# Two VectorE clears moved to GpSimd, and two ScalarE conversions moved out of the way of the second block's features, in an attention and mixture-of-experts kernel

## The chip, the cores and the metric

One core of a Trainium2 chip runs the kernel. The metric is the time of one execution on the device, in microseconds (us).

## What is computed

```
x = L0_attn_x                                   # 4 x 2048 x 256, f32
x = x + attention(layernorm(x))                 # 16 heads of 16: elu(q)+1, elu(k)+1, causal linear attention, Wo
x = x + moe(layernorm(x))                       # 8 experts, top 2 by router, hidden 512, exact gelu

# attention, token by token, with state s and z kept per batch row and head:
s = s + k_i (outer) v_i;   z = z + k_i
out_i = (q_i s) / (q_i z + 1e-6)

# moe: logits = x . router_w; top 2, softmax over the two
y = gelu(x . w1[e] + b1[e]) . w2[e] + b2[e], weighted by the two probabilities and added
```

## The kernel before, in words

The attention is done in 16 steps of 128 positions; a step holds these positions of all 4 batch rows, so 4 x 128 tokens. Every f32 operand of a matmul is split in two f16 numbers, a **high** part (ScalarE rounds it: the helpers whose names end in `hi` or `high`) and a **low** part (value minus high, on VectorE or GpSimd: `lo` or `low`), and a product is three matmuls. After the steps comes a second phase, in which gathered token rows go through their experts' two layers tile by tile; the change doesn't touch it.

Each engine runs its own program, written out by hand in the order in which it is to run, and waits on semaphores for the others. All of them walk the same list of calls (`iterations`):

```
            body(0, 0)
            body(0, 1, back=False)
            body(0, 1, front=False)
            for c in range(2, END):
                body(0, c)
```

A `body` has a **front** part, the features of step c (normalise, transpose, project to q, k and v, exponentials, splits), and a **back** part, the attention of step c-1 (scores, weighted values, state, output projection, residual, second normalisation). From c = 2 on they are interleaved. The first ones stand alone: block one is `body(0, 0)` (the features of step 0), the **second block** is `body(0, 1, back=False)` (the features of step 1), and after it stands the **back of step 0**, `body(0, 1, front=False)` with nothing of a front beside it.

What the change and the prediction name, with the lines of the kernel before:

- On ScalarE: `x_hi` (L990) copies the transposed x from the PSUM banks pF to xT. `kn_rows` (L975) copies turned k rows. `v_high` (L1024) writes the high half of v into vhl, and GpSimd's `v_low` (L1799) subtracts it and writes the low half. `w1_high` (L1048) writes the high half of one 512-column slice of the first expert weight w1 (staged in w1raw) into w1s; VectorE's `w1_low` (L1419) writes its low half. `feature_in` and `feature_exp` (L998, L999, L1004) turn a projected bank into et and lt; `qk_high` (L1017) rounds a finished feature. `turned_copies` (L1029, L1030) copies turned output weights. `score_hi` (L984) rounds a bank of scores into ahl. `out_hi` (L1035) rounds the turned attention output. `normalise` is L947.
- On VectorE: `x_lo` (L1279), `feature` (L1425), `low` (L1429), `values` (L1351, v from its bank), `score_lo` (L1274, the low half of a score bank), `norm_moments` (L1241 and L1243), `norm1_shift` (L1259 and L1260), `attention` (L1298 to L1305: denominators and the division into at), `state_part` (L1314), `residual` (L1333, L1344, L1247). Two clears stand at the end of block one: pads (L1464), which holds padding rows that are written to DRAM some 70 us later, and state (L1465), which is the attention state.
- On TensorE: `first_transposes` (L583), `project` (L564, pF from xT and was), `scores` (L650 and L654), `attend` (L669 with the state, L675 with the scores, then the state's product into pU), `out_transpose` (L695), `out_project` (L564 into pA). `attend` of step 0 waits for the cleared state (`zero_set`), for all four low score banks of its batch row (`sc_lo`) and for the low half of v (`v_lo`).
- On GpSimd: `rstd` (L1755, a power of four numbers per partition), `v_low`, `state_add` (L1783). Its start clears a part of qst (L1868).
- SyncE's queue issues the loads. The load of the second w1 slice (L493) waits for `w1_lo` of the first, since both use w1raw.

In the second block and in the back of step 0 no other front or back work lies beside these orders: in the second block ScalarE has the features alone, in the back of step 0 it has the scores.

Of the kernel before, what the change touches and what calls it, by code (L numbers as in the profile page):

```python
# [105 lines left out]
def build(nc, x, wqkvo, bqk, bv, bo, rw, w1, b1, w2, b2, cf, ch, cb, cm, out):  # L106
# [5 lines left out]
    with ExitStack() as ctx:  # L112
# [820 lines left out]
        def _(act):  # L933
# [27 lines left out]
            def body(j, c, front=True, back=True):  # L961
# [117 lines left out]
                if c == STEPS + 1:  # L1079

                    w2_high(0)
                    w2_high(1)
                if fr and c == 1:
                    v_high(0)
                    w1_high(0)
                if fr:
# [23 lines left out]
                if bk:  # L1110
                    out_hi(s, 0)
                    score_hi(1, 2)
                    score_hi(1, 3)
                if fr:
                    feature(3)
                    qk_high(2)
# [6 lines left out]
                if fr:  # L1123
                    qk_high(3)
                if bk:
                    score_hi(2, 1)
# [101 lines left out]
        def _(dve):  # L1228
            V = nc.vector
# [32 lines left out]
            def body(j, c, front=True, back=True):  # L1262
# [171 lines left out]
                if fr and c < 2:  # L1434
# [25 lines left out]
                    low(3)  # L1460
                    if c == 1:
                        w1_low(0)
                    if c == 0:
                        V.memset(pads[:].rearrange("p s d -> p (s d)"), 0.0).then_inc(pads_set, 1)  # L1464
                        V.memset(state[:].rearrange("p a b c -> p (a b c)"), 0.0).then_inc(zero_set, 1)  # L1465
                        V.tensor_copy(dummy_token[:], cfs[:, C_PAD + 2:C_PAD + PADS]).then_inc(pads_set, 1)
                        dve.wait_ge(pads_set, 1)
                        for n in range(2):
                            V.tensor_copy(pads[:, n, TOKEN:TOKEN + 1], cfs[:, C_PAD + n:C_PAD + n + 1]).then_inc(pads_set, 1)
                        dve.wait_ge(lgx0_ps, 1)  # L1470
                        logit_x(0, pR[:, LGX0:LGX0 + B * E])
# [63 lines left out]
                if ahead:  # L1535
                    norm1_stats(i + 1, 3)
                    norm_moments(i + 1, st1, mv1, ve1, (ln1_st, ln1_mv, ln1_ve))
                if c == STEPS:
                    router_slots()
# [210 lines left out]
        def _(pool):  # L1750
# [6 lines left out]
            def body(j, c, front=True, back=True):  # L1757
# [44 lines left out]
                if fr and c < 2:  # L1802

                    if c == 0:
                        rstd(1, ve1, rs1, ln1_ve, ln1_rs)
                    else:
                        v_low(0)
# [61 lines left out]
            pool.wait_ge(pow_set, 1)  # L1869
            rstd(0, ve1, rs1, ln1_ve, ln1_rs, lg[:, 0, 0:B])  # L1870
            pool.wait_ge(cf_in, 16)
            pool.wait_ge(consts_in, CONSTS)
# [75 lines left out]
```

## Time and profile before

| | |
|---|---|
| median of 3 runs | 1023.68 us (1023.34 to 1023.85) |
| profiled execution, its own time | 1024.11 us |
| its span in the trace | 1022.3 us |
| TensorE (PE) matmuls | 917.8 us, 90% of the span |
| VectorE (DVE) | 754.4 us, 74% |
| ScalarE (ACT) | 681.3 us, 67% |
| GpSimd (POOL) | 621.1 us, 61% |
| granted TensorE clock, mean | 0.976 of full speed |

Block one ends at about 25 us of the span, the second block at about 40 us, and the back of step 0 at about 65 us; the attention goes on to about 565 us. Busy time is summed over instructions and says nothing of which of them another waited for; that is read from the rows in order of time. An instruction's own duration is a little longer than the distance to the next one on its engine, since the end of one overlaps the start of the next: where instructions follow each other without a wait, one takes the distance.

### The profile page before, as it was taken

What the parts mean: (1) busy time and instruction counts of PE and PEld (TensorE: products, weight loads), DVE (VectorE), ACT (ScalarE), POOL (GpSimd) and SP (SyncE); (2) the same over time, 40 slices, a digit from 0 to 9 for tenths busy, and PEclk for the clock granted to TensorE, in tenths of its full rate; (3) what the DMA queues carried; (4) which work ended last, traced back from release to release, by engine and by line L of the source; (5) the groups of instructions that cost most, each with busy time, mean ns of one, the idle gap of its engine ahead of it and who ended that gap; (6) DMA issues with size and microseconds to landing.
All of it is one profiled execution on the core that took longest, in us unless ns stands there. A gap on an engine that the chain in (4) does not pass through costs nothing. (4 is left out here: it accounts for less than half of the span.)

```text
span 1022.3 us, 33747 instructions
## 1 busy us (share of the span) xinstructions
PE 917.8 (90%) x10786; PEld 745.5 (73%) x10787; DVE 754.4 (74%) x2281; ACT 681.3 (67%) x1296; POOL 621.1 (61%) x564
## 2 busy tenths in 40 slices
PE   6799899899989999999987659899999999999995
PEld 3577677767777677767766338678999999999994
DVE  6689788988888888888887556456666666666663
ACT  8778888888878988888875315445555555555552
POOL 2135776777677767786673644447655565656565
PEclk9999999999999999999999769999999999999998
DMA  7626744554555354644441743435655656555554
GB/s 195 199 79 204 244 129 150 153 175 125 152 150 176 125 154 142 186 132 144 141 150 47 279 137 70 68 61 96 93 97 89 98 89 98 89 98 88 95 91 51
DMA packets 102584, 131.32 MB, mean 128 GB/s; under 512 B 15056, under 2 KB 89296, under 8 KB 101648
## 3 DMA queue, kind: packets, MB, share of 16 engines
q1 hardware_dynamic: 74336, 92.54, 32.2%
q0 software_dynamic: 25680, 35.01, 18.7%
q10 hardware_dynamic: 2464, 2.38, 0.7%
q8 instruction: 65, 1.06, 0.5%
q14 instruction: 39, 0.32, 0.1%
HBM read 64.29 MB, written 65.60 MB: 127 GB/s over the span
## 5 line engine op out<-in xcount | busy, mean ns | idle before, releaser
L1906 POOL DMA_INDIRECT out<-yt,to_token x135 | 216.7, 1605 | 176.6 <-DVE yt L1744 80.2
L1274 DVE SCALAR_TENSOR_TENSOR ahl<-pS,ahl 128x512 f16<-128x512 f32 x240 | 161.2, 682 | 42.4 <-ACT ahl L984 38.4
L984 ACT ACTIVATE ahl<-pS 128x512 f16<-128x512 f32 x240 | 142.2, 599 | 49.5 <-PE pS L654 32.2
L1789 POOL DMA_INDIRECT expert_in<-xn,cur x128 | 131.6, 1028 | 30.2 <-issue 26.0
L1196 ACT ACTIVATE g<-pS,b1s 128x256 f32<-128x256 f32 (+1 forms) x140 | 57.3, 462 | 94.6 <-PE pS L564 94.6
L564 PE MATMUL pS<-gT,w1s 128*128 128x256 f16 (+1 forms) x840 | 97.3, 272 | 4.3 <-DVE gT L1703 3.5
L564 PE MATMUL pF<-w2s,ghl 128*128 x816 | 95.6, 273 | 2.4 <-issue 1.5
L1710 DVE TENSOR_TENSOR ghl<-g,ghl 128x1024 f16<-128x1024 f32 (+1 forms) x68 | 83.0, 1221 | 19.4 <-ACT ghl L1221 12.6
L564 PE MATMUL pU<-w2s,ghl 128*128 x804 | 94.2, 273 | 1.9 <-issue 1.5
L564 PE MATMUL pF<-xT,was 128*128 128x512 f16 x384 | 92.8, 379 | 3.0 <-DVE xT L1279 2.9
L1783 POOL TENSOR_TENSOR state<-state,ut 128x272 f32<-128x272 f32 x64 | 49.9, 780 | 73.4 <-DVE ut L1314 72.5
L675 PE MATMUL pO<-vhl,ahl 128*128 128x17 f16 x3072 | 90.2, 171 | 4.2 <-DVE ahl L1274 3.4
L675 PEld LDWEIGHTS pO<-vhl,ahl 128*128 128x128 f16 x3072 | 88.3, 96 | 7.4 <-DVE ahl L1274 4.2
L564 PEld LDWEIGHTS pS<-gT,w1s 128*128 x840 | 80.9, 99 | 16.1 <-issue 5.6
L654 PE MATMUL pS<-qst,kst 128*128 128x256 f16 x480 | 92.0, 274 | 0.0
L650 PE MATMUL pS<-cbs 128*128 128x384 bf16 x240 | 79.1, 329 | 11.1 <-DVE ahl L1274 7.4
L564 PEld LDWEIGHTS pF<-w2s,ghl 128*128 128x128 f16 x816 | 79.3, 98 | 13.2 <-issue 3.7
L564 PEld LDWEIGHTS pU<-w2s,ghl 128*128 128x128 f16 x804 | 78.2, 98 | 12.4 <-issue 2.9
L1196 ACT ACTIVATE g<-pO,b1s 128x256 f32<-128x256 f32 (+1 forms) x72 | 29.1, 459 | 77.4 <-PE pO L564 73.3
L1221 ACT ACTIVATE ghl<-g 128x1024 f16<-128x1024 f32 (+1 forms) x68 | 72.0, 1059 | 0.1
L564 PEld LDWEIGHTS pF<-xT,was 128*128 128x128 f16 x384 | 36.2, 98 | 35.9 <-DVE xT L1279 3.3
L654 PEld LDWEIGHTS pS<-qst,kst 128*128 128x128 f16 x480 | 47.2, 98 | 20.2 <-issue 0.3
(226 smaller groups left out, 2170.2 us busy)
## 6 DMA issues: line engine op xcount, KB each, us to landing
xg<-expert_in SPq DMA_DIRECT2D x64, 260.0 KB
qk_parts<-qkhl SPq DMA_DIRECT2D x64, 256.0 KB, 2.1
qst<-qk_parts SPq DMA_DIRECT2D x192, 64.0 KB
kst<-qk_parts SPq DMA_DIRECT2D x96, 128.0 KB
xs<-x SPq DMA_DIRECT2D x16, 512.0 KB
out<-x SPq DMA_DIRECT2D x16, 512.0 KB
w1raw<-w SPq DMA_DIRECT2D x16, 256.0 KB
w2raw<-w SPq DMA_DIRECT2D x4, 1024.0 KB, 7.2
```

The source lines that it names most:

```text
L564: mm = nc.tensor.matmul(out, lhs(a, k), rhs(b_, k), start=(t == 0 and not go_on), stop=(t == len(terms) - 1))
L650: nc.tensor.matmul(o[:].rearrange("p (h q) -> p h q", q=C)[:, :, 0:STACK], ident16, mask_first, start=True, stop=False, skip_group_check=True)
L654: mm = nc.tensor.matmul(o[:, e * 2 * C:(e + 1) * 2 * C], kst[:, sp_, pr, b * C:(b + 1) * C], qst[:, sp_, :, pr, b * C:(b + 1) * C], start= ...
L675: mm = nc.tensor.matmul(pO[:, h * VC:(h + 1) * VC], ahl[:, b % 2, a, h * C:(h + 1) * C], vhl[:, sp_, b_, b, h * VC:(h + 1) * VC], start=False,
L984: nc.scalar.activation(ahl[:, b % 2, 0, n * 4 * C:(n + 1) * 4 * C], score_bank(fr, n)[:], ACT.Relu).then_inc(sc_hi, 1)
L1196: nc.scalar.activation(g[:, p1, f, h * P:h * P + width], hidden[p1][f // 2][:, c0:c0 + width], ACT.Gelu, bias=b1s[:, bass.ds(e * FC + f, 1 ...
L1221: nc.scalar.activation(ghl[:, p1, 0, :, 0:n], g[:, p1, :, 0:n], ACT.Copy).then_inc(g_hi, 1)
L1274: V.scalar_tensor_tensor(ahl[:, b % 2, 1, cols], score_bank(fr, n)[:], 0.0, ahl[:, b % 2, 0, cols], ALU.max, ALU.subtract).then_inc(sc_lo, 1)
L1710: V.tensor_tensor(ghl[:, p1, 1, :, 0:n], g[:, p1, :, 0:n], ghl[:, p1, 0, :, 0:n], ALU.subtract).then_inc(g_lo, 1)
L1783: G.tensor_tensor(sb_, sb_, ut[:, b % 2], ALU.add).then_inc(state_new, 1)
L1789: G.indirect_dma_start(xg_dram, bass.IndirectOffsetOnAxis(ap=cur[:, qp, 2 * b + t:2 * b + t + 1], axis=0), xn2[:, qp, b], None).then_inc(s ...
L1906: G.indirect_dma_start(out, bass.IndirectOffsetOnAxis(ap=to_token[:, c % 2, s:s + 1], axis=0), yt[:, c % 2, s], None, compute_op=ALU.add). ...
```

## The change

In the second block, ScalarE's `v_high(0)` goes from ahead of the first `feature_in` to the end of the block, behind the last `qk_high`. `w1_high(0)` leaves the block and stands in the back of step 0, behind `score_hi(1, 3)`. VectorE's `w1_low(0)` goes from the end of the second block to the back of step 0, behind the `norm_moments` of step 2's first normalisation and ahead of `score_lo(2, 0)`. The two clears leave VectorE: GpSimd clears pads behind its first `rstd` and state behind its second, and VectorE's copies into the pads wait for the clear ahead of the first of them.

```
--- before.py
+++ after.py
@@ -1080,9 +1080,6 @@
 
                     w2_high(0)
                     w2_high(1)
-                if fr and c == 1:
-                    v_high(0)
-                    w1_high(0)
                 if fr:
                     feature_in(0)
                 if bk:
@@ -1111,6 +1108,8 @@
                     out_hi(s, 0)
                     score_hi(1, 2)
                     score_hi(1, 3)
+                if c == 1 and not front:
+                    w1_high(0)
                 if fr:
                     feature(3)
                     qk_high(2)
@@ -1122,6 +1121,8 @@
                     normalise(1, 0)
                 if fr:
                     qk_high(3)
+                if fr and c == 1:
+                    v_high(0)
                 if bk:
                     score_hi(2, 1)
                 if fr and c >= 2:
@@ -1458,13 +1459,9 @@
                     low(2)
                     values(1)
                     low(3)
-                    if c == 1:
-                        w1_low(0)
                     if c == 0:
-                        V.memset(pads[:].rearrange("p s d -> p (s d)"), 0.0).then_inc(pads_set, 1)
-                        V.memset(state[:].rearrange("p a b c -> p (a b c)"), 0.0).then_inc(zero_set, 1)
+                        dve.wait_ge(pads_set, 1)
                         V.tensor_copy(dummy_token[:], cfs[:, C_PAD + 2:C_PAD + PADS]).then_inc(pads_set, 1)
-                        dve.wait_ge(pads_set, 1)
                         for n in range(2):
                             V.tensor_copy(pads[:, n, TOKEN:TOKEN + 1], cfs[:, C_PAD + n:C_PAD + n + 1]).then_inc(pads_set, 1)
                         dve.wait_ge(lgx0_ps, 1)
@@ -1535,6 +1532,8 @@
                 if ahead:
                     norm1_stats(i + 1, 3)
                     norm_moments(i + 1, st1, mv1, ve1, (ln1_st, ln1_mv, ln1_ve))
+                if c == 1 and not front:
+                    w1_low(0)
                 if c == STEPS:
                     router_slots()
                     norm2_shift()
@@ -1803,6 +1802,7 @@
 
                     if c == 0:
                         rstd(1, ve1, rs1, ln1_ve, ln1_rs)
+                        G.memset(state[:].rearrange("p a b c -> p (a b c)"), 0.0).then_inc(zero_set, 1)
                     else:
                         v_low(0)
                     return
@@ -1868,6 +1868,7 @@
             G.memset(qst[0:STACK, 0].bitcast(F32).rearrange("p a b c -> p (a b c)"), 0.0).then_inc(qst_zero, 1)
             pool.wait_ge(pow_set, 1)
             rstd(0, ve1, rs1, ln1_ve, ln1_rs, lg[:, 0, 0:B])
+            G.memset(pads[:].rearrange("p s d -> p (s d)"), 0.0).then_inc(pads_set, 1)
             pool.wait_ge(cf_in, 16)
             pool.wait_ge(consts_in, CONSTS)
             iterations(pool, body)
```

What the engines now run, at three places. The rows are instructions in program order, with the semaphores that they wait for in brackets.

ScalarE, the start of the second block and its end, before (L990 is `x_hi`, L975 `kn_rows`, L1024 `v_high`, L1048 `w1_high`, L998 the first half of `feature_in`, L1017 `qk_high`, L1029 and L1030 `turned_copies`, L984 `score_hi`):

```order
L990 ACTIVATE xT<-pF 128x512 [waits v_ps,xT_ps] x2
L975 ACTIVATE kn<-pU 128x2x512 [waits kn_ps]
L1024 ACTIVATE vhl<-v 128x1088 [waits v_done]
L1048 ACTIVATE w1s<-w1raw 128x512 [waits w1_in]
L998 ACTIVATE et<-pF,negb 128x512 [waits qk_f,qk_ps]
...
L1017 ACTIVATE qkhl<-kf 128x512 [waits part_out3,qk_f]
L1029 ACTIVATE ahl<-pA 128x512 [waits turned_ps]
L1030 ACTIVATE ahl<-pR 128x256
L984 ACTIVATE ahl<-pS 128x512 [waits sc_ps] x2
```

The same two places in the changed program:

```order
L990 ACTIVATE xT<-pF 128x512 [waits v_ps,xT_ps] x2
L975 ACTIVATE kn<-pU 128x2x512 [waits kn_ps]
L998 ACTIVATE et<-pF,negb 128x512 [waits qk_f,qk_ps]
...
L1017 ACTIVATE qkhl<-kf 128x512 [waits part_out3,qk_f]
L1024 ACTIVATE vhl<-v 128x1088 [waits v_done]
L1029 ACTIVATE ahl<-pA 128x512 [waits turned_ps]
L1030 ACTIVATE ahl<-pR 128x256
L984 ACTIVATE ahl<-pS 128x512 [waits sc_ps] x2
```

`v_high` has moved behind the features and stands ahead of the step's first `score_hi`; `w1_high` is gone from here.

VectorE, end of block one and start of the second, before (L1429 is the last `low` of block one, L1279 is `x_lo`):

```order
L1429 TENSOR_TENSOR qkhl<-kf,qkhl 128x512 [waits qk_hi]
L1464 MEMSET pads 128x520
L1465 MEMSET state 128x1088
L1466 COPY dummy_token<-cfs 128x16
L1469 COPY pads<-cfs 128x1 [waits pads_set]
L1469 COPY pads<-cfs 128x1
L1324 TENSOR_TENSOR lgx<-pR,sd 128x32 [waits sd1_done,lgx0_ps]
L1279 TENSOR_TENSOR xT<-pF,xT 128x512 [waits xT_hi] x2
```

And in the changed program, where line numbers are one higher up to the clears:

```order
L1430 TENSOR_TENSOR qkhl<-kf,qkhl 128x512 [waits qk_hi]
L1464 COPY dummy_token<-cfs 128x16 [waits pads_set]
L1466 COPY pads<-cfs 128x1 x2
L1325 TENSOR_TENSOR lgx<-pR,sd 128x32 [waits sd1_done,lgx0_ps]
L1280 TENSOR_TENSOR xT<-pF,xT 128x512 [waits xT_hi] x2
```

The two clears are gone from between block one and `x_lo`; the three small copies stay.

VectorE, back of step 0, in the changed program (L1253, L1242 and L1244 are the statistics and moments of step 2's first normalisation, L1420 is `w1_low`, L1275 `score_lo(2, 0)`, L1334 to L1248 the residual of batch row 0, L1299 the start of `attention(1)`):

```order
L1253 BN_STATS st<-xs 128x6 [waits x_in]
L1242 BN_AGGR mv<-st 128x2 [waits ln1_st]
L1242 BN_AGGR mv<-st 128x2 x3
L1244 TENSOR_REDUCE ve<-mv 128x4 [waits ln1_mv]
L1420 SCALAR_TENSOR_TENSOR w1s<-w1raw,w1s 128x512 [waits w1_hi]
L1275 SCALAR_TENSOR_TENSOR ahl<-pS,ahl 128x512 [waits sc_hi]
L1334 TENSOR_TENSOR lga<-pA,lgx 128x8 [waits lgx_done,wo_ps]
L1345 SCALAR_TENSOR_TENSOR x<-pA,xs 128x256
L1248 BN_STATS st<-x 128x6 [waits x1_done]
L1299 TENSOR_SCALAR rden<-pO 128x16 [waits o_ps]
```

Before, the row of `w1_low` is not there; it stood between the second block's last `low` and `score_lo(0, 0)`, some 20 rows earlier.

## Rows read from the trace of the kernel before

**Rows 1.** Timeline (start, us, engine, line; idle before and releaser in brackets), VectorE, end of block one.

```profile
26.04 0.96 DVE L1465 MEMSET state<- 128x1088 f32 x1 [0.17 <-issue]
...
27.16 1.27 DVE L1279 TENSOR_TENSOR xT<-pF,xT 128x512 f16<-128x512 f32 x2
```

**Rows 2.** Timeline, start of the second block, ScalarE, TensorE and GpSimd.

```profile
25.91 1.09 ACT L990 ACTIVATE xT<-pF 128x512 f16<-128x512 f32 x2 [0.42 <-PE pF L583]
...
27.79 1.12 ACT L1024 ACTIVATE vhl<-v 128x1088 f16<-128x1088 f32 x1
27.90 2.76 PE L564 MATMUL pF<-xT,was 128*128 128x512 f16 x12 [1.46 <-DVE xT L1279]
28.79 0.64 ACT L1048 ACTIVATE w1s<-w1raw 128x512 f16<-128x512 f32 x1
28.99 2.25 POOL L1799 TENSOR_TENSOR vhl<-v,vhl 128x1088 f16<-128x1088 f32 x1 [10.63 <-ACT vhl L1024]
29.40 0.69 ACT L998 ACTIVATE et<-pF,negb 128x512 f32<-128x512 f32 x1
```

**Rows 3.** Timeline, step 2, one wait of ScalarE for TensorE and one of VectorE for ScalarE.

```profile
70.02 0.60 ACT L984 ACTIVATE ahl<-pS 128x512 f16<-128x512 f32 x1
...
70.22 1.46 PE L564 MATMUL pF<-xT,was 128*128 128x512 f16 x6
...
70.65 0.69 DVE L1274 SCALAR_TENSOR_TENSOR ahl<-pS,ahl 128x512 f16<-128x512 f32 x1 [0.44 <-ACT ahl L984]
...
71.71 0.69 ACT L998 ACTIVATE et<-pF,negb 128x512 f32<-128x512 f32 x1 [0.48 <-PE pF L564]
```

**Rows 4.** Timeline, end of the second block and first scores, all engines.

```profile
39.83 0.58 ACT L1029 ACTIVATE ahl<-pA 128x512 f32<-128x512 f32 x1
...
40.57 1.09 ACT L984 ACTIVATE ahl<-pS 128x512 f16<-128x512 f32 x2
...
40.97 0.68 DVE L1419 SCALAR_TENSOR_TENSOR w1s<-w1raw,w1s 128x512 f16<-128x512 f32 x1
...
41.58 1.28 DVE L1274 SCALAR_TENSOR_TENSOR ahl<-pS,ahl 128x512 f16<-128x512 f32 x2
...
44.11 1.40 PE L675 MATMUL pO<-vhl,ahl 128*128 128x17 f16 x48 [0.55 <-DVE ahl L1274]
```

**Rows 5.** Timeline, middle of the back of step 0, all engines.

```profile
50.85 0.60 ACT L984 ACTIVATE ahl<-pS 128x512 f16<-128x512 f32 x1 [1.51 <-PE pS L654]
...
51.78 0.68 DVE L1274 SCALAR_TENSOR_TENSOR ahl<-pS,ahl 128x512 f16<-128x512 f32 x1
51.95 1.02 POOL L1755 TENSOR_TENSOR rs<-ve,cfs 128x4 f32<-128x4 f32 x1 [4.29 <-DVE ve L1243]
...
54.20 0.44 PE L695 MATMUL pA<-cfs,at 128*128 128x128 f32 x2 [0.98 <-DVE at L1305]
...
62.46 1.38 PE L675 MATMUL pO<-vhl,ahl 128*128 128x17 f16 x48 [0.85 <-DVE ahl L1274]
```

**Rows 6.** Timeline, GpSimd's first work and VectorE's beside it.

```profile
1.31 3.51 POOL L1868 MEMSET qst<- 96x4096 f32 x1 [0.43 <-DVE v L1235]
...
8.55 0.16 DVE L1259 SCALAR_TENSOR_TENSOR sh<-mv,rs 128x4 f32<-128x4 f32 x1 [1.24 <-POOL rs L1755]
...
16.79 0.69 DVE L1425 TENSOR_TENSOR qf<-et,lt 128x512 f32<-128x512 f32 x1
17.04 1.32 POOL L1755 TENSOR_TENSOR rs<-ve,cfs 128x4 f32<-128x4 f32 x1 [8.52 <-DVE ve L1243]
```

**Rows 7.** Timeline, step 2, VectorE beside a GpSimd subtraction.

```profile
76.07 1.16 POOL L1776 TENSOR_TENSOR qkhl<-qf,qkhl 128x512 f16<-128x512 f32 x1 [0.65 <-ACT qkhl L1017]
76.12 1.13 DVE L1292 SCALAR_TENSOR_TENSOR sh<-mv,rs 128x4 f32<-128x4 f32 x1
```

**Rows 8.** Windows: us, PE, PEld, DVE, ACT, POOL busy (instructions), PEclk, DMA share, GB/s.

```profile
41.50:45.00 3.50, 2.95 (x53) 2.67 (x53) 3.47 (x9) 1.73 (x4) 0.00 (x0) 1.00 0.64 182
45.00:48.10 3.10, 3.10 (x35) 2.47 (x32) 1.70 (x6) 0.87 (x2) 0.76 (x1) 0.50 0.37 98
```

More of the change, by code:

```diff
@@ L1082, in body @@
                     w2_high(1)
-                if fr and c == 1:
-                    v_high(0)
-                    w1_high(0)
                 if fr:
@@ L1113, in body @@
                     score_hi(1, 3)
+                if c == 1 and not front:
+                    w1_high(0)
                 if fr:
@@ L1124, in body @@
                     qk_high(3)
+                if fr and c == 1:
+                    v_high(0)
                 if bk:
@@ L1460, in body @@
                     low(3)
-                    if c == 1:
-                        w1_low(0)
                     if c == 0:
-                        V.memset(pads[:].rearrange("p s d -> p (s d)"), 0.0).then_inc(pads_set, 1)
-                        V.memset(state[:].rearrange("p a b c -> p (a b c)"), 0.0).then_inc(zero_set, 1)
+                        dve.wait_ge(pads_set, 1)
                         V.tensor_copy(dummy_token[:], cfs[:, C_PAD + 2:C_PAD + PADS]).then_inc(pads_set, 1)
-                        dve.wait_ge(pads_set, 1)
                         for n in range(2):
@@ L1537, in body @@
                     norm_moments(i + 1, st1, mv1, ve1, (ln1_st, ln1_mv, ln1_ve))
+                if c == 1 and not front:
+                    w1_low(0)
                 if c == STEPS:
@@ L1805, in body @@
                         rstd(1, ve1, rs1, ln1_ve, ln1_rs)
+                        G.memset(state[:].rearrange("p a b c -> p (a b c)"), 0.0).then_inc(zero_set, 1)
                     else:
@@ L1870, in _ @@
             rstd(0, ve1, rs1, ln1_ve, ln1_rs, lg[:, 0, 0:B])
+            G.memset(pads[:].rearrange("p s d -> p (s d)"), 0.0).then_inc(pads_set, 1)
             pool.wait_ge(cf_in, 16)
```

## The prediction

> **What bounds the kernel now.** The page says first that TensorE is busy for 90% of the span, VectorE for 74% and ScalarE for 67%. Over 1022 us that describes the steady part; everything that the change touches lies in the first 65 us, and it moves or removes a handful of instructions of 0.5 to 1.1 us. So the shares decide nothing here. I read the timeline of all engines from 5 to 70 us, asking at each place that the diff names which wait ended last, and how long the engine on which an instruction is put had been waiting.
>
> In the second block ScalarE is the bound: from its x_hi at 25.91 on it has hardly a gap until 39 us, and TensorE and VectorE wait for it. The block's first feature_in, at 29.40, looks as if it came late because v_high and w1_high stand ahead of it. They take 27.79 to 29.40 [rows 2]. But feature_in also needs the first projection, whose matmuls start at 27.90, and that start waited 1.46 us for VectorE's x_lo [rows 2]. Where ScalarE plainly waits for such a projection, it starts 1.49 us after the first matmul (70.22 to 71.71) [rows 3]; 27.90 + 1.49 is 29.39. So the two conversions fill a wait that is there anyway, to within 0.01 us. What holds the projection is x_lo at 27.16, which comes late because VectorE is still at the two clears, the second of them from 26.04 for 0.96 us, and at four small instructions behind them [rows 1].
>
> At the block's end two chains meet in the scores of batch row 0. ScalarE's score_hi starts at 40.57; score_lo could follow 0.63 later (70.02 to 70.65, where VectorE waits for it [rows 3]), at 41.20. It starts at 41.58, right behind w1_low at 40.97 [rows 4]: VectorE is the later one by 0.38. Four score_lo back to back then release TensorE's attend at 44.11, which waited 0.55 for them [rows 4].
>
> In the back of step 0, TensorE, VectorE and ScalarE take turns. The wait that matters is at 54.20: the turn of batch row 1's attention output waited 0.98 us for VectorE's division, and VectorE runs from score_lo(2, 0) at 51.78 to there without a gap [rows 5]. ScalarE in contrast had 1.51 us idle ahead of 50.85 [rows 5].
>
> **The change part by part.**
>
> The clears leave VectorE. x_lo then waits for x_hi alone: 25.91 + 0.63 [rows 2, 3] gives 26.54 in place of 27.16, so the projection starts 0.62 earlier, at 27.28. The clears are longer than that together; the rest is not gained, because VectorE would be waiting for x_hi.
>
> v_high and w1_high leave the start of the block. This removes 1.61 us of ScalarE's work (27.79 to 29.40 [rows 2]) but puts a wait in its place: the projection, started at 27.28, releases feature_in at 27.28 + 1.49 = 28.77. The gain on ScalarE is 29.40 - 28.77 = 0.63, the same 0.6 us as above and not a second one. The block's features are a chain through ScalarE, so its last qk_high ends and turned_copies could start at 39.83 - 0.63 = 39.20.
>
> v_high comes back there: 1.00 us (27.79 to 28.79 [rows 2]). score_hi(0, 0) starts at 40.57 - 0.63 + 1.00 = 40.94, which is 0.37 **later** than before, and score_lo(0, 0) can start at 40.94 + 0.63 = 41.57. VectorE, rid of w1_low and itself 0.6 earlier, is free well ahead of that. Before it was 41.58. The chain has changed hands from VectorE to ScalarE, and the time is the same to 0.01: **0.0 us**. Behind v_high stand turned_copies and all scores on ScalarE, which is why this spot is not free; v_low behind it on GpSimd starts 1.20 after v_high (27.79 to 28.99) and takes 2.25 [rows 2], so it ends at 39.20 + 3.45 = 42.65, ahead of attend's 44.11 by 1.4 us.
>
> w1_high goes into the 1.51 us in which ScalarE waited for scores [rows 5]: its 0.61 costs nothing; without that cover it would cost 0.61.
>
> w1_low goes ahead of score_lo(2, 0), and there nothing covers it. It takes 0.61 (40.97 to 41.58 [rows 4]). Behind it on VectorE are score_lo(2, 0), the residual and attention(1), and TensorE waits for the last of these at 54.20 already. So this wait grows from 0.98 to 1.59, and with it the rest of the step moves: **+0.61 us**. From there I find nothing that gives it back; the next long wait, at 62.46, is for score_lo behind score_hi behind TensorE's own scores [rows 5]. The load of the second w1 slice starts some 1.4 us later (it waits for w1_low), and its reader comes 11 us after that.
>
> The clears on GpSimd: its qst clear takes 3.51 us for 4096 numbers per partition [rows 6], 0.86 ns each. So pads (520) is about 0.45 us and state (1088) about 0.93 (an estimate from that row). They follow the rstd that ends at 8.51 and the one that ends at 18.36; the next work on GpSimd is at 17.04 and, now, 40 us [rows 6]. The work that hides them is none, GpSimd is idle, and the readers come 17 and 24 us later. Cost 0, unless they hold VectorE; that is a rival below.
>
> Sum: 0.0 + 0.61 = 0.6 us slower. The profiled execution took 1024.11, 0.43 more than the median of the runs; I put the sum on the median: 1023.68 + 0.61 = **1024.3 us**. A measurement of this kernel tells differences from about 0.2% on, 2.05 us, so this counts as no change.
>
> **A rule beside the rows.** Two engines share something in SBUF: a VectorE instruction on 128x4 took 1.13 us beside a GpSimd subtraction that had started 0.05 us ahead of it [rows 7], where its like takes 0.16 [rows 6]; and where VectorE's addition had started first, it kept its 0.69 and GpSimd's rstd took 1.32 in place of 1.02 [rows 5, 6]. What starts first is not disturbed, the other one waits. No row shows a clear on GpSimd beside such an instruction.
>
> The Trainium skill, SBUF — State Buffer, "Who interferes with whom", says that a VectorE instruction with two SBUF inputs contends with a GpSimd instruction that reads SBUF, but not with one that only writes it, and that the second to start blocks for the whole of the first. By that a clear holds nobody and the sum stays at 0.6. The trace agrees with the second half (1.13 against 0.16); the first half no row here shows.
>
> **The rivals.**
>
> (a) The two chains at the scores don't tie: ScalarE's is shorter than I reckon, VectorE's 0.6 shows, and it pays for w1_low. Bounds: between nothing and 0.6 gained. Time 1023.7. For it: the tie rests on two latencies of 0.63. Against: both are read from waits.
>
> (b) The half-clock stretch goes. From 45.0 to 48.1 the granted clock is 0.50, so 1.2 of 2.4 GHz, after 3.5 us in which TensorE was busy for 2.95 [rows 8]. Work that took 3.1 us there is about 1.55 at full clock. If TensorE's changed waits leave the clock up, that is 0.61 - 1.4 (a little of the 1.55 is waited off), or 1022.9. If other such stretches later in the attention go too, the kernel is faster by over 2 us.
>
> (c) rstd wins over w1_low. Both follow norm_moments. w1_low is ready at 51.78 and rstd starts at 51.95 [rows 5]: 0.17 us of margin. If rstd is first, w1_low waits to 52.97, and score_lo(2, 0) starts at 53.58, 1.8 late: 1025.5. For it: the price is that of [rows 7]. Against: nothing between the reduction and w1_low waits.
>
> (d) The clears hold VectorE after all. norm1_shift's two-input instruction starts at 8.55, as the pads clear does, and the same happens 10 us on with the state clear. It would be held 0.45 and 0.93 us, on the way to the first normalise and to the block's x_hi: 0.6 + 1.3 = 1.9, so 1025.6. Against: the GpSimd instruction of [rows 7] reads two operands from SBUF, a clear none; that keeps the chance small. The Trainium skill's rule above would exclude it.
>
> (e) The one that ends slower: the wait at 54.20 has a half-clock stretch behind it. TensorE's idle time there goes from 0.98 to 1.59 us, and TensorE then runs nearly without a gap to 61 us, on the path. A stretch like that of [rows 8] at that place loses half of 3.1 to 3.4 us, 1.6 to 1.7. With the 0.6 it is 2.3: 1026.0, over the bound of 1025.7. It decides if the idle time is long enough to bring the clock down; a stretch in which TensorE was busy for 84% did it once [rows 8].
>
> That the change doesn't do what it says is not open: the orders of the instructions show each move.
>
> **How the numbers follow.** My forecast 0.50; (a) 0.14; (b) 0.08 with one stretch and 0.05 with more; (c) 0.08; (d) 0.05; (e) 0.10. The predicted time is that of the forecast, 1024.3, its own range 1024.0 to 1024.7 for the spread of the runs. The range over the cases goes from (b) with one stretch, 1022.9, to (d), 1025.6, and leaves out (e) and the rest of (b), 0.15. Faster by over 0.2%: 0.05. Slower: (e), 0.10. Within: 0.85.
>
> **What would show it.** x_lo at about 26.5, the first projection at 27.3 after a shorter wait than 1.46, feature_in at 28.8 with ScalarE idle for about 1 us ahead of it; v_high at about 39.2, score_hi(0, 0) at 40.9, score_lo(0, 0) at 41.6 now waiting for ScalarE, attend at 44.1 as before; w1_low of 0.6 to 0.7 us at about 51.8, rstd longer than 1.02, TensorE's turn at 54.8 after a wait of 1.6. Wrong would be: attend earlier than 43.9 (a), w1_low over 1 us long (c), norm1_shift over 0.3 us long (d), a granted clock of 0.5 between 50 and 60 us (e), or none of it between 45 and 48 (b).

## The result and the profile after

The changed kernel is slower: median 1025.51 us of 20 executions (1022.46 to 1029.56), against 1023.26 us of 20 of the kernel before on the same chip (1019.64 to 1026.47). The ratio is 1.0025, with a 95% interval of 1.0015 to 1.0034, so between 1.5 and 3.5 us; the means lie 2.62 ± 1.02 us apart.

The one profiled execution of the change does not show this. It took 1022.46 us, the quickest of the 20, with a span of 1020.5 us, and the one of before took 1024.11. Most of this difference lies in the expert phase, which the change doesn't touch: 680 to 700 us in each, in windows (columns as in [rows 8]), first before, then after.

```profile
680.00:700.00 20.00, 16.25 (x145) 13.82 (x143) 9.67 (x25) 9.34 (x18) 11.47 (x11) 1.00 0.50 80
```

```profile
680.00:700.00 20.00, 18.21 (x164) 15.58 (x162) 11.13 (x29) 9.35 (x19) 11.31 (x11) 1.00 0.57 86
```

TensorE is busy for 2.0 us less in the first: it waited twice for VectorE's gT, 1.89 and 1.86 us, in the second once, 1.79. Two single traces are therefore no measurement of this change; only the stretch from the second block to step 2 is compared below, counted from the block's first `x_hi`.

The places of the prediction, in the timeline after the change, all engines:

```profile
26.03 1.08 ACT L990 ACTIVATE xT<-pF 128x512 f16<-128x512 f32 x2 [0.42 <-PE pF L583]
26.66 1.29 DVE L1280 TENSOR_TENSOR xT<-pF,xT 128x512 f16<-128x512 f32 x2 [1.00 <-ACT xT L990]
...
27.41 2.76 PE L564 MATMUL pF<-xT,was 128*128 128x512 f16 x12 [0.86 <-DVE xT L1280]
28.92 0.69 ACT L998 ACTIVATE et<-pF,negb 128x512 f32<-128x512 f32 x1 [0.88 <-PE pF L564]
...
39.33 1.09 ACT L1024 ACTIVATE vhl<-v 128x1088 f16<-128x1088 f32 x1
...
41.08 1.08 ACT L984 ACTIVATE ahl<-pS 128x512 f16<-128x512 f32 x2
...
41.70 1.29 DVE L1275 SCALAR_TENSOR_TENSOR ahl<-pS,ahl 128x512 f16<-128x512 f32 x2 [1.14 <-ACT ahl L984]
...
44.24 1.39 PE L675 MATMUL pO<-vhl,ahl 128*128 128x17 f16 x48 [0.64 <-DVE ahl L1275]
...
51.90 0.68 DVE L1420 SCALAR_TENSOR_TENSOR w1s<-w1raw,w1s 128x512 f16<-128x512 f32 x1
52.06 1.39 POOL L1754 TENSOR_TENSOR rs<-ve,cfs 128x4 f32<-128x4 f32 x1 [4.29 <-DVE ve L1244]
...
54.92 0.44 PE L695 MATMUL pA<-cfs,at 128*128 128x128 f32 x2 [1.58 <-DVE at L1306]
```

Here the block begins 0.12 us later than in [rows 2], so times are taken from its `x_hi`. `feature_in` comes 2.89 us behind it (before 3.49) and now waits 0.88 for the projection. `score_hi(0, 0)` comes at 15.05 (14.66), `score_lo(0, 0)` at 15.67 (15.67 [rows 4]) and waits for ScalarE, no longer for `w1_low`. `attend` comes at 18.21 (18.20). The turn at 54.92 waits 1.58 us (0.98 [rows 5]) and comes at 28.89 (28.29). Up to here what the sum says happens, to 0.03 us. By it the kernel would be 0.6 us slower, and it is 2.3 by the medians and 2.6 by the means of 20.

GpSimd's clears, in the timeline of 8 to 19 us after the change:

```profile
8.48 0.52 POOL L1871 MEMSET pads<- 128x520 f32 x1
8.54 0.16 DVE L1260 SCALAR_TENSOR_TENSOR sh<-mv,rs 128x4 f32<-128x4 f32 x1 [1.24 <-POOL rs L1754]
...
18.30 1.00 POOL L1805 MEMSET state<- 128x1088 f32 x1
18.37 0.16 DVE L1260 SCALAR_TENSOR_TENSOR sh<-mv,rs 128x4 f32<-128x4 f32 x1 [0.90 <-POOL rs L1754]
```

A VectorE instruction with two SBUF inputs starts 0.06 and 0.07 us behind the start of a clear and takes 0.16 us, as it did alone [rows 6].

### The profile page after: what moved, and what is told of

The parts are those of the page before. It is cut to its first block and busy times, and to the rows that moved or that the text cites. A ratio compares the mean times of both kernels' runs of the same rounds, so it can differ in the third digit from the quotient of the medians.

```text
span 1020.5 us, 33747 instructions
## 1 busy us (share of the span) xinstructions
PE 918.2 (90%) x10786; PEld 745.7 (73%) x10787; DVE 753.3 (74%) x2279; ACT 680.8 (67%) x1296; POOL 620.9 (61%) x566
## 3 DMA queue, kind: packets, MB, share of 16 engines
q8 instruction: 65, 1.06, 0.4%
## 5 line engine op out<-in xcount | busy, mean ns | idle before, releaser
L1275 DVE SCALAR_TENSOR_TENSOR ahl<-pS,ahl 128x512 f16<-128x512 f32 x240 | 161.2, 682 | 43.2 <-ACT ahl L984 38.8
L984 ACT ACTIVATE ahl<-pS 128x512 f16<-128x512 f32 x240 | 142.1, 599 | 48.8 <-PE pS L654 32.6
L1798 POOL TENSOR_TENSOR vhl<-v,vhl 128x1088 f16<-128x1088 f32 x16 | 35.9, 2244 | 46.5 <-ACT vhl L1024 44.4
```

What stands on the lines that cost most here:

```text
L984: nc.scalar.activation(ahl[:, b % 2, 0, n * 4 * C:(n + 1) * 4 * C], score_bank(fr, n)[:], ACT.Relu).then_inc(sc_hi, 1)
L1275: V.scalar_tensor_tensor(ahl[:, b % 2, 1, cols], score_bank(fr, n)[:], 0.0, ahl[:, b % 2, 0, cols], ALU.max, ALU.subtract).then_inc(sc_lo, 1)
```

## The experiments

Each comparison is of 12 executions (11 in the last) with 23 to 35 of the kernel before on the same chip. "Difference" is that of the means, with 1.96 standard errors. "At half clock" is the time that an execution spends at 1.2 GHz. It is worked out from the difference in mean granted clock c as 2 x (1 - c) x the time, since a stretch at 1.2 GHz counts half; each such difference has an error of 1.4 to 3.8 us. The runs came in four groups, each on one chip, on which the kernel before took 1020.5, 1023.2, 1019.2 and 1024.1 us in the mean, so numbers are compared within a group.

Theory H: `w1_low` costs its 0.6 to 0.7 us, and TensorE's longer wait for it brings a stretch at half clock behind it, which costs 1 to 2 us more. Theory W: the work moved costs this alone, somewhere that the sum missed. Theory N: there is no more than the 0.6, and the rest is the spread of the measurement. In the expectations of the first four runs A is N, B is H, and C is that executions differ by the timing of the expert phase. C isn't tested by any run; the two traces above differ so at 680 to 700 us, and C says of no part of the change why it should be slower in the mean.

### The change again, and its parts alone

**The change as it is.**

> The changed kernel once more, unaltered. Theory A (only w1_low on the path counts): step 1 starts (x_hi of step 2's features) at 66.2 to 66.4 us of the span as in the first trace, and the median lies 0.6 us above before. Theory B (the moved waits bring TensorE to half clock more often): the median lies 2 us or more above before, and the slow executions have a mean granted clock lower by 0.0017 for each further stretch of 3.4 us at half clock than the 0.975 of the quick ones, with 1 to 1.5 us lost per stretch. Theory C (the executions differ by the phase of the expert tiles' scatters): times spread over 4 us or more at one and the same clock, and the stretch between the first row_prob and the last scatter differs by 2 us from trace to trace.

Ratio 1.0022 (1.0009 to 1.0036), difference +2.03 ± 0.99. The slowdown repeats on another chip. In this trace there are two stretches at half clock; windows:

```profile
45.59:49.00 3.41, 3.41 (x39) 2.65 (x36) 2.01 (x7) 1.05 (x3) 0.76 (x1) 0.50 0.32 88
49.00:55.83 6.83, 4.57 (x83) 3.76 (x82) 6.54 (x22) 2.68 (x5) 1.40 (x1) 1.00 0.63 166
55.83:59.24 3.41, 3.41 (x43) 2.49 (x42) 2.40 (x6) 1.58 (x3) 0.76 (x1) 0.50 0.00 0
```

The first is the one that the kernel before has too [rows 8]. The second is new: it begins 0.35 us behind the turn (55.48, which waited 1.58 us), and TensorE has no gap in it, so what it loses is on the path.

**The w1 moves alone**, in the kernel before (both calls are put where the change has them; the lines below show only where they leave):

```
                 if fr and c == 1:
                     v_high(0)
-                    w1_high(0)
...
-                    if c == 1:
-                        w1_low(0)
```

> Before with w1_high and w1_low alone moved to the back of step 0; the clears and v_high stay. Theory A: score_lo(0, 0) is freed of w1_low but waits for ScalarE, 0.38 us earlier than before (41.2 us); w1_low at about 51.5 then costs 0.61, so the features of step 2 start at 65.8 us, 0.2 later than before's 65.59, and the median is 0.2 us above. Theory B: TensorE's wait for the turn of batch row 1 is 1.6 us as with the change, and the clock is as low and the time as long as with the change, 2 us above before.

Ratio 1.0000 (0.9984 to 1.0015), difference +0.54 ± 1.24. Without `w1_low` ahead of the scores, `attend` comes 17.74 us behind `x_hi`, some 0.4 earlier than before (18.11 to 18.20 in its traces); the turn waits 1.58 us and comes at 27.73, against 27.50 in the trace of before that has no half-clock stretch either ahead of it. So w1 alone gains some 0.4 at the scores and pays 0.6 at the turn. Behind the turn this trace has its only stretch at half clock in this part (from 54.20). The expectation of B, 2 us above before, is missed: the interval ends at 1.78. The trace itself is at step 2 0.7 us behind the mean of before's, which the interval holds.

**The change without its w1 part** (w1_high and w1_low back in their old places, `v_high` at the end, clears on GpSimd):

```
+                if fr and c == 1:
+                    w1_high(0)
                 if fr:
                     feature_in(0)
...
+                    if c == 1:
+                        w1_low(0)
```

> The change without its w1 part: clears on GpSimd, v_high at the end of the second block, w1_high ahead of the first feature_in and w1_low at the end of the block as before. Theory A: the scores tie as in the change (attend at 44.1 to 44.2) and nothing is added later, so the features of step 2 start at 65.6 to 65.7 us and the median equals before's within 0.1 us. Theory B: TensorE's wait is 0.98 again and the clock and the median are before's, within what the runs tell. Theory C: the median may differ from before by 1 us with no difference ahead of the expert tiles.

Ratio 0.9994 (0.9978 to 1.0010), difference -0.19 ± 1.15: clears and `v_high` alone are not shown to cost anything. This speaks for `w1_low`'s place; but its one trace speaks against the simple form of H. It has a stretch at half clock from 56.97 although the turn waited only 0.90 us there. A 1.58 us wait is not needed for one.

**A version meant to be faster than both**: clears on GpSimd, `v_high` back ahead of `feature_in`, `w1_high` behind `score_hi(1, 0)`, `w1_low` behind `state_part(0)`:

```
+                if fr and c == 1:
+                    v_high(0)
                 if fr:
                     feature_in(0)
...
                     score_hi(1, 0)
+                if c == 1 and not front:
+                    w1_high(0)
...
                     state_part(0)
+                if c == 1 and not front:
+                    w1_low(0)
```

> Clears on GpSimd; v_high back ahead of the first feature_in, where ScalarE waits for the projection anyway; w1_high behind score_hi(1, 0) and w1_low behind state_part(0), where each engine waited (3.26 and 0.80 us). Theory A: features of the second block 0.6 us earlier, score_lo(0, 0) at 40.6 in place of 41.6, attend at 43.1, features of step 2 at 64.6 us, 1.0 us ahead of before; median 1.0 us below before. Theory B: no wait of TensorE is longer than before, so the clock is before's and the gain is this 1.0.

Ratio 0.9990 (0.9974 to 1.0006), difference -0.90 ± 1.25. `attend` comes at 17.22, the turn at 27.00 after a wait of 0.97, and there is no half-clock stretch up to step 2, which begins 38.38 us behind the block.

### Keeping TensorE busy

These kernels leave the order of the work alone and put matmuls into TensorE's waits, whose result nobody reads.

**The change again**, as the partner on this chip.

> The changed kernel, unaltered, as the partner of the next two on the same chip. If it is half-clock stretches: 2 us above before again, mean granted clock 0.001 to 0.002 below that of before's executions, and a trace that shows a stretch at half clock behind TensorE's 1.6 us wait at 55 us in some phases of the stretches and not in others. If only the 0.6 us of w1_low counts and the rest is the spread of the runs: 0.6 us above.

Ratio 1.0017 (1.0003 to 1.0031), difference +1.65 ± 1.10. Half-clock stretches from 43.42 (6.83 us long) and from 57.07.

**Eight matmuls of 256 columns ahead of the turn of batch row 1:**

```
+                if first_s and bk:
+                    keep_busy(8)
                 if bk:
                     out_transpose(s, 1)
```

> The change, with 8 matmuls of 256 columns whose result nobody reads, about 0.9 us at full clock, in TensorE's wait ahead of the turn of batch row 1 (1.6 us). They lie inside the wait, so by themselves they neither cost nor give anything. Half-clock theory: with TensorE busy there the stretches behind 55 us become rare; the median falls by 0.5 to 1.2 us against the change, and the clock rises by 0.0005 to 0.0017. Theory of w1_low alone: no difference to the change.

Ratio 1.0014 (1.0001 to 1.0028), difference +0.83 ± 1.29: not conclusive by its time. In its trace the stretch behind the turn is gone, the one at the scores (42.85) is not. The other executions don't confirm it by their clock: they spend 3.6 us more at half clock than before, the change beside them 4.3, and the two differ by 0.7 ± 3.5. That filling this one wait is enough is therefore not shown.

**Four more ahead of `attend` of batch row 0:**

```
+                    if first_s and b == 0:
+                        pe.wait_ge(kn_done, 2)
+                        keep_busy(4, pU)
                     pe.wait_ge(sc_lo, 4 * g + 4)
```

> As the run before, and 4 more such matmuls, 0.45 us, in TensorE's 0.64 us wait ahead of the first attend at 44 us. Half-clock theory: the stretch from 45 us, which costs 1.4 us and which both kernels had in their first traces, becomes rare too; features of step 2 at 64.9 us in a trace without a stretch, and the median 1 to 2.5 us below the change. Theory of w1_low alone: no difference to the change.

Ratio 0.9997 (0.9985 to 1.0010), difference -0.31 ± 1.00. Against the change on the same chip it is 1.96 ± 1.28 us faster, by work that computes nothing. TensorE at the turn, in its timeline:

```profile
52.81 1.04 PE L661 MATMUL pR<-cbs 128*128 128x256 bf16 x8
54.55 0.44 PE L703 MATMUL pA<-cfs,at 128*128 128x128 f32 x2 [0.71 <-DVE at L1316]
```

The wait of 1.58 us is filled but for 0.71; `w1_low` is where it was, and the turn comes no earlier by it. The clock stays up:

```profile
40.00:50.00 10.00, 8.08 (x108) 6.29 (x108) 8.14 (x21) 6.62 (x13) 3.00 (x2) 1.00 0.58 169
50.00:62.00 12.00, 11.08 (x195) 9.31 (x193) 11.02 (x33) 5.89 (x12) 2.72 (x3) 1.00 0.23 61
```

**The same matmuls in the kernel before:**

> The kernel before with the same 4 and 8 matmuls in its waits of 0.55 and 0.98 us. Half-clock theory: the stretch from 45 us becomes rare, up to 1.4 us below before; the difference between the change and before, both kept busy, is then the 0.6 us of w1_low alone. Otherwise: no difference to before.

Ratio 1.0015 (1.0003 to 1.0028), difference +0.71 ± 0.77. Its block to step 2 takes 38.89 us, as long as that of the kernel before where it has no stretch (38.88, below), so the filling itself costs nothing there. What this run gives is a clean price at the turn: it comes 27.50 us behind `x_hi` here, 28.20 in the change with the same matmuls. Of these 0.70 us, 0.61 lie between `attend` and the turn (9.38 and 9.99 us), and that is `w1_low`. The other 0.09 lie ahead of `attend` (18.12 and 18.21), where before's own traces spread by as much (18.11 to 18.20).

Both expectations of the whole time are missed. The kernel before didn't get faster, and the change kept busy, expected 0.6 us slower than this kernel, was 1.02 ± 1.02 us faster. The price at the turn is not seen in the whole here; see step 3 below.

### How often the stretches come

**The kernel before against itself**, and one more execution of it:

> The kernel before, unaltered, against itself: the ratio shows what these comparisons make of no difference, 1.0000 within 0.0015. Its trace shows the first 70 us at another phase of the half-clock stretches. Theory of the half clock: none or one stretch in the first 70 us, and where there is one, about 1.3 us from the start of the second block to step 2's features for it: 38.4 us with none, 39.7 with one.

> The kernel before, one look: again 38.4 us from the second block to step 2's features with no half-clock stretch, 39.7 with one; if it comes to 41 us or more with two, as in two of three traces of the change, then the stretches don't tell the two kernels apart.

Ratio 0.9994 (0.9981 to 1.0006), difference -0.47 ± 1.19, as it should be. The first trace has no half-clock stretch between 40 and 62 us, the second has one, from 45.37. Without a stretch the block to step 2 takes 38.88 us and not the 38.4 expected, so the stretch at the scores costs 0.8 us and not 1.3. By the clock this kernel came out 1.7 us less at half clock than itself, which shows the error of that measure.

**The change, a single execution:**

> The changed kernel, one look: 39.1 to 39.6 us from the second block to step 2's features with no half-clock stretch, 40.3 with one, 41.3 to 41.8 with two or a double one. Half-clock theory: more often two than one.

Half-clock stretches from 44.17 and from 57.83, 1.85 us behind the turn.

**The version of `e4_best` again:**

> The arrangement with v_high in ScalarE's wait and both w1 pieces in idle time, a second time: 38.4 us from the second block to step 2's features, and 0.5 to 1.5 us below before. If the first result (0.9 below) was chance: within 0.5 us of before.

Ratio 1.0002 (0.9986 to 1.0018), difference -0.01 ± 1.49. Block to step 2 38.37, no stretch. The gain at this place repeats to 0.01 us and the gain of the whole doesn't: 0.5 to 1.3 us ahead of before's traces at step 2, and by step 5 the mean lead is 0.2 (140.05 us from the block against 140.22 in two and three traces). It isn't shown to be faster than before.

Step 3 alone takes 33.8 to 36.5 us in the 17 traces (33.79 to 35.46 in before's, 35.39 to 35.55 in the change's, 35.3 to 36.5 in those of the kernels kept busy, of this version and of the next one). In all of them VectorE waits there for a load of x rows (xs), for 1.40 to 2.53 us, and TensorE waits behind it; in the kernel before:

```profile
114.25 0.75 DVE L1252 BATCH_NORM_STATS2 st<-xs 128x6 f32<-128x256 f32 x2 [2.21 <-DMA xs<-x]
...
115.38 0.31 PE L564 MATMUL pA<-worh,aT 128*128 128x8 f16 x6 [2.73 <-DVE aT L1319]
```

In 15 of the 17 a half-clock stretch begins between 1.1 us before the end of TensorE's wait and 1.4 us behind it, and the trace with the shortest step 3 has none. What is won or lost by step 2 is therefore not yet what the whole wins or loses. This is also where the trace of the kernel before kept busy loses its lead: 38.89 us to step 2, but 140.93 to step 5, 0.7 behind the mean of before's three traces. One trace doesn't show that its other executions do the same.

**The change with `w1_high` behind `score_hi(1, 0)` and `w1_low` behind `state_part(0)`, nothing else:**

> The change with its two w1 pieces alone in other places: w1_high behind score_hi(1, 0), w1_low behind state_part(0), where ScalarE and VectorE waited (3.3 and 0.8 us). v_high stays late and the clears stay on GpSimd. TensorE's wait ahead of the turn of batch row 1 is 0.98 in place of 1.58 us. Both theories: at least the 0.7 us of w1_low comes back. Half-clock theory: the stretches behind 55 us become rare too and the median is 1.5 to 2.2 us below the change, level with before. Theory of w1_low alone: 0.7 below the change.

Ratio 0.9999 (0.9986 to 1.0013), difference -0.72 ± 1.00. The turn waits 0.97 us and comes at 27.99, 0.21 earlier than with `w1_low` in the change's place (28.20), so this is not a free place either and the 0.7 expected back doesn't come back at the turn; but no stretch follows in this trace. Against the change on the same chip it is 1.66 ± 1.18 us faster, much more than 0.21.

**The change and the change kept busy, again:**

> The change as the partner on the same chip: 1.6 to 2.3 us above before, its mean granted clock 0.001 to 0.002 lower, and 41.3 to 41.8 us from the second block to step 2's features if its trace has two stretches.

> The change kept busy in both waits, a second time: no half-clock stretch in its trace between 40 and 60 us, 39.6 us from the second block to step 2's features, a mean clock at or above before's, and 1.3 to 2 us below the change. If the first result was chance: level with the change.

The change: 1.0007 (0.9993 to 1.0022), +0.93 ± 1.06, the smallest of its four comparisons. Kept busy: 1.0000 (0.9986 to 1.0014), -0.06 ± 1.23, so 1.0 ± 1.4 below the change, less than the 1.3 to 2 expected and by itself not told from nothing. The trace of this change shows the price at its largest. Windows from the turn of batch row 1 to the next turn, first in the kernel before, then here:

```profile
54.20:60.71 6.51, 6.34 (x115) 5.32 (x116) 5.92 (x17) 3.75 (x8) 0.76 (x1) 1.00 0.00 0
```

```profile
54.67:63.73 9.06, 9.06 (x116) 7.06 (x116) 6.07 (x17) 3.98 (x8) 0.76 (x1) 0.63 0.00 0
```

The same matmuls, 2.55 us longer. A stretch of 6.83 us began at 54.52, within the wait of 1.58 us:

```profile
50.00:54.52 4.52, 3.08 (x67) 2.62 (x65) 4.23 (x16) 1.19 (x2) 1.40 (x1) 1.00 0.68 201
54.52:61.35 6.83, 6.68 (x56) 5.00 (x57) 4.66 (x14) 2.85 (x6) 0.76 (x1) 0.50 0.00 0
```

### The traces side by side

All from the timelines, in us. "Turn" is that of batch row 1's attention output ([rows 5], 54.20); the next turn is that of batch row 2; the last column is from the block's `x_hi` to that of step 2. Lengths are 3.41 us where none stands.

| trace | half-clock stretches from 40 to 62 us | to attend | to the turn | turn to next turn | to step 2 |
|---|---|---|---|---|---|
| before | 44.99 | 18.20 | 28.29 | 6.51 | 39.68 |
| before, third | 45.37 | 18.18 | 28.26 | 6.52 | 39.65 |
| before again | none | 18.11 | 27.50 | 6.50 | 38.88 |
| change | 45.32 | 18.21 | 28.89 | 6.51 | 40.28 |
| change again | 45.59, 55.83 | 18.22 | 28.92 | 7.48 | 41.29 |
| change, third | 43.42 (6.83), 57.07 | 18.21 | 28.97 | 7.98 | 41.83 |
| change, fourth | 44.17, 57.83 | 18.20 | 28.56 | 8.03 | 41.47 |
| change, fifth | 54.52 (6.83) | 18.21 | 28.20 | 9.06 | 42.13 |
| w1 only | 54.20 | 17.74 | 27.73 | 7.48 | 40.09 |
| no w1 | 43.31 (6.83), 56.97 | 18.22 | 28.37 | 8.17 | 41.43 |
| change, busy late | 42.85 | 18.21 | 28.52 | 6.50 | 39.91 |
| change, busy at both, two traces | none | 18.21 | 28.20 | 6.51 | 39.59 |
| before, busy at both | none | 18.12 | 27.50 | 6.51 | 38.89 |
| best, two traces | none | 17.22 | 27.00 | 6.50 | 38.38 |
| change, w1 in idle | none | 18.21 | 27.99 | 6.50 | 39.38 |

What is seen in it: turn to next turn takes 6.50 to 6.52 us wherever the clock stays up, and 7.5 to 9.1 where it doesn't, and what is lost is still there at step 2. Of the five traces of the change four have a stretch there, of the three of before none. Sorted by TensorE's wait ahead of the turn, over all kernels without filling: with 1.47 to 1.58 us (the change, w1 only) five of six traces have a stretch behind it, with 0.90 to 0.98 us one of seven. Chance alone would sort them so in about one case of 40. The mean to step 2 is 41.40 for the change and 39.40 for before, a difference of 2.00. It is made up of 0.70 at the turn (0.61 of it `w1_low`) and of the stretches behind the turn, (0 + 0.97 + 1.47 + 1.52 + 2.55) / 5 = 1.30. The stretch at the scores cancels: 0.5 us in the mean in both. Filling both waits takes away 1.30 + 0.5 = 1.8 us by this table, and of these 0.5 is a loss that the kernel before has too. By step 5 the means are 142.65 us for the change, 140.22 for before, 141.26 for the change kept busy and 141.73 (one trace) for w1 in idle.

The executions without a trace say the same of the change by their granted clock, which lies 4.3 ± 1.6 us at half clock from before over the three groups; the traces have 4.5 us more between 40 and 62 us (6.8 against 2.3 in the mean). The single rows carry the errors named above, so that the 3.2 of "w1 only" and "no w1" are not told from nothing:

| kernel | difference to before, us | at half clock, us more than before |
|---|---|---|
| change, three groups | +2.03, +1.65, +0.93 | +3.9, +4.3, +4.3 |
| change, busy late | +0.83 ± 1.29 | +3.6 |
| change, busy at both, two groups | -0.31, -0.06 | -2.5, -1.9 |
| change, w1 in idle | -0.72 ± 1.00 | +0.4 |
| w1 only | +0.54 ± 1.24 | +3.2 |
| no w1 | -0.19 ± 1.15 | +3.2 |
| before, busy at both | +0.71 ± 0.77 | -0.6 |
| best, two groups | -0.90, -0.01 | +0.7, -3.2 |
| before again | -0.47 ± 1.19 | -1.7 |

Over the first 20 executions of the change, those that were at half clock 1 us longer took 0.26 us longer (slope -0.53 us per 0.001 of clock, which is 2.05 us at half clock; correlation -0.70); over all 276 later ones, each kernel about its own mean, it is 0.21. So 4.2 us more at half clock are worth 0.9 to 1.1 us, and with the 0.70 at the turn that gives 1.6 to 1.8. The four comparisons of the change, weighted by their errors, give 1.83 ± 0.52. That 2.00 at step 2, this estimate and the whole agree is support, not proof: step 3 alone differs by up to 2.7 us between traces.

## Why the prediction was wrong

**The sum of the moves held.** Clears off VectorE: projection and `feature_in` 0.61 and 0.60 earlier behind `x_hi`, forecast 0.62 and 0.63. The conversions filled a wait: `feature_in` gained no second time. The hand-over at the scores: `score_hi(0, 0)` later by 0.39 (forecast 0.37), `score_lo(0, 0)` level, so 0.0. `w1_high` free. Clears on GpSimd free: 0.52 and 1.00 us long, with nobody behind them. `w1_low`: forecast +0.61, measured 0.60 in the first trace and 0.61 from `attend` to the turn between the two kernels kept busy.

**The step that failed** is the one that says of the turn: "this wait grows from 0.98 to 1.59, and with it the rest of the step moves: +0.61 us. From there I find nothing that gives it back". The wait was priced at its own length. What was missing is what TensorE's work behind it costs: 1.30 us in the mean, twice the term itself. The forecast had this as rival (e), at the right place and with 2.3 us in all, beside 2.25 measured between the medians; its mistake was the chance, 0.10, where four of five traces show it. One stretch cost 1.0 to 1.5 us in the change's traces, less than the 1.7 given there; that the total fits is partly because one trace in five had a double one and one had none.

Why so low a chance? The prediction writes down no argument against (e). What spoke against it was that in the one trace TensorE kept its clock behind 0.98 us of waiting. The kernel before shows from the start that this is no firm sign: it lost its clock at 45 us after a stretch with 2.95 of 3.50 us busy [rows 8], and kept it at 56 us with less, in windows of the first trace:

```profile
52.00:56.00 4.00, 2.85 (x53) 2.07 (x50) 3.72 (x11) 1.92 (x4) 1.73 (x2) 1.00 0.42 99
56.00:60.00 4.00, 4.00 (x92) 3.74 (x89) 3.62 (x12) 2.21 (x5) 0.00 (x0) 1.00 0.00 0
```

Two places of about the same kind, one down and one up in the one execution seen: I read that as a place at the edge, which the change moved over it; the counts above bear this out, but no run measured an edge. Treating one trace's clock as if each execution had the same was the error in (e), and in (b) too: the stretch at 45 us did not go with the change; it comes and goes by itself, in two of three traces of before and four of five of the change. The range, 1022.9 to 1025.6, reached the measured median by 0.1 us and only because (d) had its upper end there.

**The other rivals.** (a) fell: attend at 18.20 and 18.21. (c) fell by little: `w1_low` at 51.90, `rstd` 0.16 us behind it, and it is `rstd` that was held, 1.39 us long where it took 1.02. (d) fell: 0.16 us beside both clears. (b) did not happen in the first trace: its stretch begins at 45.32. At (c) and (d) the rule named in the prediction, of the Trainium skill, SBUF — State Buffer, "Who interferes with whom", held in its direction: a GpSimd instruction that only writes held no one, and the second to start, `rstd` behind `w1_low`, was the one that waited. That the second waits for the whole of the first is not what this row shows: `w1_low` still ran for 0.52 us when `rstd` began, and `rstd` became 0.37 us longer.

**Theories.** N falls: the change is slower in the comparison of 20 and in two of the three later ones, each interval above zero, the third +0.93 ± 1.06. W falls as the whole: with `w1_low` in the same place and TensorE kept busy, the time is that of before (-0.31 ± 1.00 and -0.06 ± 1.23), and against the change on the same chips it is less by 1.96 ± 1.28 and 1.0 ± 1.4, weighted 1.5 ± 0.9, with 6.9 ± 3.2 and 6.3 ± 2.5 us less at half clock. Some 0.5 us of this is the stretch at the scores, which before has too, so that the level with before is not by itself proof. The run that doesn't share this weakness is w1 in idle: only the two w1 pieces move, 0.21 us comes back at the turn, 4.0 ± 2.8 us less are spent at half clock, and the whole is 1.66 ± 1.18 us faster than the change. H holds in its size; the place behind the turn is shown by the traces alone, since filling that wait alone gave no clear result. It does not hold as "a wait of 1.58 us brings the stretch": the first trace of the change has the wait and no stretch, and the change without w1 has a stretch behind a wait of 0.90. The wait raises how often it comes.

**What stays open.** Why the change without w1 is level with before while it spends 3.2 us more at half clock (by the slopes above that is 0.7 to 0.8 us, within its ± 1.15, so it may be chance). Why the kernel before, kept busy, is 0.7 us over before and 1.02 ± 1.02 over the change kept busy: its trace loses its lead in step 3, but what makes step 3 as long as it is was not worked out. And what else of TensorE's work beside the wait decides in which execution the stretch comes; no run here varied the wait alone in fine steps.

## What to carry to other kernels

Price a wait that you lengthen ahead of unbroken TensorE work at its own length plus the clock's: here 0.7 us of conversion on VectorE cost 2, and the same conversion put where TensorE's wait stayed at 0.97 us cost nothing that can be measured. Where a half-clock stretch shows in one trace, look at several executions before giving it a place or a chance, and compare the mean granted clock of all of them: over three groups of 12 it told 4.3 ± 1.6 us at half clock, where single times spread by 7 us; one group alone can be off by 2 to 4. And count to a mark behind the change (here step 2) to see what the change does there, but don't take it for the gain of the whole: here a wait for a load in step 3 set the traces apart by up to 2.7 us.

## What the runs showed of the hardware

- The stretches at 1.2 GHz are 3.41 us long or twice that in this part, and begin at other times in each execution, from 42.85 to 45.59 and from 54.20 to 57.83 us, though the second block starts within 2 us of the same time in all traces (25.88 to 27.81). One began within TensorE's wait (54.52, the turn at 54.67), one 1.85 us behind its end (57.83, the turn at 55.98).
- 3.41 us at 1.2 GHz cost 1.0 to 1.7 us behind the turn, where TensorE had no gap, and 0.3 to 0.8 us at the scores, where TensorE waits for VectorE in any case.
- Twelve matmuls that compute nothing, in two waits of one step, left no stretch between 40 and 62 us in three traces (of the change and of before) and gave the change back 1.5 ± 0.9 us; to the kernel before they gave nothing (+0.71 ± 0.77).
- In step 3 a load holds VectorE for 1.40 to 2.53 us and TensorE behind it for 1.92 to 3.05, and in 15 of 17 traces a stretch at 1.2 GHz begins within that wait or up to 1.4 us behind it.
